# Side products between the score blocks, weighted sums in pairs: reordering one tile of an adaLN attention and expert block

## What is computed

```python
h = _layernorm(x) * (1 + ca) + sa
x = x + ga * _L0_attn_ref(h, Wqkv, bqkv, Wo, bo)          # 16 heads of 8 channels
h = _layernorm(x) * (1 + cb) + sb
x = x + gb * _L0_ffn_ref(h, router_w, expert_weights)     # 8 experts, the best 2 per token

# attention: qkv is reshaped (not transposed) to (B, 16, S, 24)
scores = jnp.einsum('bhsd,bhtd->bhst', q, k) * (1.0 / math.sqrt(hd))
attn = jax.nn.softmax(scores, axis=-1)
vals = jnp.einsum('bhst,bhtd->bhsd', attn, v)
# experts: all eight products are formed, the two best are weighted and summed
out = ((combined + remap_bias) * weights).sum(axis=0)
```

## Time and profile before

| what | value |
|---|---|
| median of 3 runs | 594.01 us (593.64 to 594.24) |
| the profiled execution: its own time | 592.45 us |
| its span, first to last instruction | 590.7 us |
| TensorE busy | 542.7 us, 92% |
| ScalarE busy | 487.3 us, 83% |
| VectorE busy | 341.5 us, 58% |
| GpSimd busy | 219.3 us, 37% |
| mean granted TensorE clock | 0.98 |

### The profile page before, as it was taken

The page is one execution under the profiler, slowest core; times in us unless marked ns, Lnnn a source line. Parts: engine busy times, 40 slices in busy tenths (PEclk is TensorE's granted clock), DMA queues, the critical chain, the costliest instruction groups (busy, mean ns, idle before and its releaser), DMA issues.

```text
span 590.7 us, 14331 instructions
## 1 busy us (share of the span) xinstructions
PE 542.7 (92%) x4046; PEld 202.0 (34%) x4046; DVE 341.5 (58%) x1276; ACT 487.3 (83%) x546; POOL 219.3 (37%) x436
## 2 busy tenths in 40 slices
PE   7499999999999999999999999999999999999944
PEld 5233323333333333333333333333333323333222
DVE  4325566656566666656565656556656666554564
ACT  1389998989888989998989899898989898989700
POOL 1103333333344432343444433333444333433347
PEclk9999999999999999999999999999999999999966
DMA  4383333333233333332233333332333332322000
GB/s 96 96 221 80 80 92 93 84 90 86 70 79 87 85 89 85 90 79 72 72 87 87 85 85 91 83 75 69 85 87 83 85 94 71 85 72 78 22 18 13
DMA packets 85496, 48.43 MB, mean 82 GB/s; under 512 B 61508, under 2 KB 76240, under 8 KB 85456
## 3 DMA queue, kind: packets, MB, share of 16 engines
q1 hardware_dynamic: 84400, 47.43, 31.9%
q10 hardware_dynamic: 1056, 0.46, 0.4%
HBM read 32.91 MB, written 14.94 MB: 81 GB/s over the span
## 4 chain that ended last, share of the span: by engine, by line
PE 59%; ACT 18%; DVE 9%; issue 7%; SPq 2%; POOL 2%; DVEq 2%; DMA 1%; POOLq 0%; ACTq 0%
PE ps_attn L673 20%; ACT probs L522 18%; PE ps_scores L655 16%; PE ps_side L703 9%; PE ps_side L590 4%; DVE sums_inv L980 2%; PE ps_side L597 2%; DVE attn L974 1%; PE ps_side L686 1%; DVE weighted L1060 1%; PE ps_side L584 1%; PE ps_side L682 1%; DVEq L949 1%; PE ps_side L606 1%; PE ps_side L690 1%
## 5 line engine op out<-in xcount | busy, mean ns | idle before, releaser
L522 ACT ACTIVATE probs<-ps_scores 128x1024 f32<-128x1024 f32 x512 | 482.6, 1030 | 68.4 <-PE ps_scores L655 66.2
L673 PE MATMUL ps_attn<-probs,values 128*32 128x512 f32 x2048 | 273.8, 607 | 2.9 <-DVE attn L974 2.9
L655 PE MATMUL ps_scores<-query_stack,key_stack 32*128 32x512 f32 x1024 | 133.5, 500 | 17.7 <-ACT probs L522 4.1
L655 PEld LDWEIGHTS ps_scores<-query_stack,key_stack 32*128 32x128 f32 x1024 | 51.7, 183 | 172.1 <-ACT probs L522 139.8
L411 POOL TENSOR_SCALAR var_eps<-moments 128x1 f32<-128x1 f32 x64 | 12.3, 193 | 247.4 <-DVE moments L991 222.2
L703 PE MATMUL ps_side<-experts_gated,h2T 128*128 (+2 forms) x228 | 75.6, 413 | 0.0
L673 PEld LDWEIGHTS ps_attn<-probs,values 128*32 128x32 f32 x2048 | 40.6, 108 | 67.6 <-issue 57.0
L913 DVE TENSOR_TENSOR qkT<-ps_side,bqk_cols 128x256 f32<-128x256 f32 x32 | 13.6, 425 | 58.8 <-PE ps_side L703 46.5
L1060 DVE TENSOR_TENSOR weighted<-ps_side,coef 128x128 f32<-128x128 f32 (+1 forms) x114 | 46.5, 407 | 1.4 <-PE ps_side L703 1.4
L974 DVE COPY attn<-ps_attn 128x512 f32<-128x512 f32 x32 | 22.1, 691 | 38.3 <-PE ps_attn L673 37.6
L936 DVE TENSOR_REDUCE norm_max<-ps_side 128x1 fp32r<-128x32 f32 x31 | 5.9, 191 | 63.7 <-PE ps_side L703 61.1
(11 more groups left out here) (119 smaller groups left out, 503.0 us busy)
## 6 DMA issues: line engine op xcount, KB each, us to landing
key_stack<-k_scr SPq DMA_DIRECT2D x128, 128.0 KB, 2.7
query_stack<-q_scr SPq DMA_DIRECT2D x124, 64.0 KB, 2.3
q_scr<-qk_parts SPq DMA_DIRECT2D x186, 32.0 KB, 2.0
k_scr<-qk_parts SPq DMA_DIRECT2D x64, 64.0 KB, 1.7
a_scr<-attn SPq DMA_DIRECT2D x128, 18.0 KB
sums<-a_scr SPq DMA_DIRECT2D x32, 64.0 KB, 2.1
attnT<-a_scr SPq DMA_DIRECT2D x32, 64.0 KB, 2.3
out_dram<-out_all SPq DMA_DIRECT2D x32, 64.0 KB, 1.7
```

What stands on the lines that cost most here:

```text
L522: nc.scalar.activation(probs[:, k % RING, g, :], ps_scores[:, slot(parity, k, g), :], ACT.Exp, scale=SCALE)\
L655: mm = nc.tensor.matmul(out_, key_stack[p0:p0 + 32, parity, 2 * k:2 * k + 2, :].rearrange("p j r -> p (j r)"), query_stack[p0:p0 + 32, par ...
L673: mm = nc.tensor.matmul(ps_attn[q:q + 32, :], values[:, parity, g, k, :], probs[:, k % RING, g, h * HALF:(h + 1) * HALF], start=(k == 0), ...
```

## The change

It changes the order in which TensorE goes through a tile, and what depends on that order:

- scores(0) stand alone at the start; then for k = 0, 2, 4, 6: the side group, scores(k+1), both weighted sums k-2 and k-1, and scores(k+2). The side groups thus stand behind the scores of even blocks, and two `weigh` follow each other behind those of odd ones.
- the values of a tile are projected in side1 and no longer in side2 (`a_project_v` with the bank's second quarter), and VectorE reads them there.
- the experts are in four pieces of two.
- on VectorE `c_save` moves from the start of the tile to behind `c_router_top`, and `c_vals` from its end to ahead of the readers of side3.
- on ScalarE the router's exponential comes behind block 0 and no longer behind block 1.

```diff
-    PIECES = ((0, 1), (1, 3), (3, 5), (5, 8))
+    PIECES = ((0, 2), (2, 4), (4, 6), (6, 8))
...
-                    if k == 1 and before >= 3:
+                    if k == 0 and before >= 3:
                         router(plus(act, t, -2))
...
                 if past < 2 <= before:
                     c_transpose(ps, at[-1])
+                if before >= 2 and after >= 1:
+                    a_project_v(at[2], 1 - parity, P)
...
-            def two_blocks(at, parity, before, k0, exact):
-
-                for k in (k0, k0 + 1):
-                    scores(at[0], at[1], parity, k, exact)
-                    if k >= 2:
-                        weigh(at[0], at[1], parity, k - 2)
+            def between_sides(at, parity, before, k, exact):
+
+                scores(at[0], at[1], parity, k, exact)
+                for past_k in (k - 3, k - 2):
+                    if past_k >= 0:
+                        weigh(at[0], at[1], parity, past_k)
                     elif before:
-                        weigh(at[-1], at[0], 1 - parity, KT - 2 + k)
+                        weigh(at[-1], at[0], 1 - parity, KT + past_k)
+                if k + 1 < KT:
+                    scores(at[0], at[1], parity, k + 1, exact)
...
                 with pe.Else():
                     pe.sem_inc(m_scores, M_PE)
-                for k0 in range(0, KT, 2):
-                    with pe.If(flag == 0):
-                        two_blocks(at, parity, before, k0, True)
-                    with pe.Else():
-                        two_blocks(at, parity, before, k0, False)
-                    if k0 == 0:
+                    scores(at[0], at[1], parity, 0, False)
+                for k in range(0, KT, 2):
+                    if k == 0:
                         drained3(at, before, after, 0)
                         side0(ps_side, at, batch, parity, before, after, 0)
...
+                    with pe.If(flag == 0):
+                        between_sides(at, parity, before, k + 1, True)
+                    with pe.Else():
+                        between_sides(at, parity, before, k + 1, False)
...
-                if past < 1 <= before:
+                if after < 0 and past < 1:
                     c_save(t)
...
                 if past < 3 <= before:
                     c_router_top(at[-2])
-
-                written1(at, before, past)
+                if after >= 0 and before:
+                    c_save(t)
+
+                written1(at, before, after, past)
...
                 if after >= 2:
                     a_qk_parts(at[2], at[3])
+                if after >= 0 and before:
+                    c_vals(t)
```

More of the change, by code:

```diff
@@ L591, in a_project_qk, with a_project_v @@
                 mm.then_inc(ev["qk_ps_done"], 1)
-            def a_project_v(u1, ring):
+            def a_project_v(u1, ring, col):
                 for n in range(G):
                     for odd in range(2):
-                        mm = nc.tensor.matmul(ps_side[odd * R:(odd + 1) * R, 2 * P + n * R:2 * P + (n + 1) * R],
+                        mm = nc.tensor.matmul(ps_side[odd * R:(odd + 1) * R, col + n * R:col + (n + 1) * R],
                                               hT[:, ring, n * R:(n + 1) * R], wvT[:, odd].rearrange("p k d -> p (k d)"),
@@ L746, in drained1 @@
                     reached(pe, ev["h2T_done"], at[-1])
+                if before >= 2 and after >= 1:
+                    reached(pe, ev["values_done"], at[2])
                 if past < 4 <= before:
@@ L753, in side2 @@
                     a_project_qk(at[3], parity)
-                if after >= 1:
-                    a_project_v(at[2], 1 - parity)
+                if before < 2:
+                    a_project_v(at[2], 1 - parity, 2 * P)
                 if past < 3 <= before:
@@ L803, in tile @@
                     exact_maxima(t, parity)
+                    scores(at[0], at[1], parity, 0, True)
                 with pe.Else():
                     pe.sem_inc(m_scores, M_PE)
-                for k0 in range(0, KT, 2):
-                    with pe.If(flag == 0):
-                        two_blocks(at, parity, before, k0, True)
-                    with pe.Else():
-                        two_blocks(at, parity, before, k0, False)
-                    if k0 == 0:
+                    scores(at[0], at[1], parity, 0, False)
+                for k in range(0, KT, 2):
+                    if k == 0:
                         drained3(at, before, after, 0)
                         side0(ps_side, at, batch, parity, before, after, 0)
-                    if k0 == 2:
+                    if k == 2:
                         drained0(at, before, after, 0)
@@ L1069, in written0, with written1 @@
                     reached(dve, ev["normT_done"], at[2])
-            def written1(at, before, past):
+            def written1(at, before, after, past):
                 if past < 4 <= before:
                     reached(dve, experts_done[3], at[-3])
+                elif before >= 2 and after >= 1:
+                    reached(dve, ev["v_ps_done"], at[2])
             def written2(at, before, after, past):
@@ L1079, in written2 @@
                     reached(dve, experts_done[0], at[-2])
-                elif after >= 1:
+                elif before < 2:
                     reached(dve, ev["v_ps_done"], at[2])
+                elif after >= 2:
+                    reached(dve, ev["qk_ps_done"], at[3])
             def written3(at, before, after, past):
@@ L1134, in tile @@
                     c_weigh(banks[1], at[-3], parity, 3)
+                if before >= 2 and after >= 1:
+                    a_values(at[2], 1 - parity, P)
                 if past < 3 <= before:
@@ L1142, in tile @@
                     a_qk(at[3])
-                if after >= 1:
-                    a_values(at[2], 1 - parity)
+                if before < 2:
+                    a_values(at[2], 1 - parity, 2 * P)
                 if past < 3 <= before:
```

12 lines of the change are left out of this document (6 added, 6 removed).

## The result

The change makes the kernel faster: 586.23 us (median of 4 runs, 586.05 to 587.36) against 594.12 us (4 runs of before, 593.64 to 596.58) beside it. The ratio is 0.9863, with an interval of 0.9833 to 0.9893. The profiled execution took 587.36 us, the longest of the four, and its span is 585.6 us.

The account below looks back on a forecast made before the run. TensorE and ScalarE hold each other up in turn, so a chain bounds the kernel. Twelve turns at 0.81 (9.7) plus 1.1 for tiles 28 and 29 make 10.8 off 594.01: 583.2 us, range 579 to 588 (0.45).

Parts of the forecast that it names:

- The chain of a pair, 1.62 + 2.29: TensorE and ScalarE: even scores to odd 1.62 unless the side group exceeds 1.19, odd to even 2.29; a pair 3.91.
- the rival of the cheap switch: TensorE: second weigh passes to scores in 0.86, not 1.00, giving 571 us; larger gain, 567 to 579, had chance 0.22.
- The copy: Copy out of `ps_attn` behind VectorE's router chain: weigh(0) at 6.24 (odd) and 7.00 (even), costing 0.28 in odd tiles.
- Head 1 and the register instructions: Even tile's first step: ScalarE's late head 1 makes it 1.84, register instructions behind scores(0) add 0.32, giving 2.16.
- Side1: TensorE's side group with the value projection added and one expert fewer: 1.14 long, hidden under ScalarE's first head.
- What stays hidden: Claimed x1hat ready for side1 (4.8 against 4.88 in even tiles), side2's inputs in time, and `c_vals` waiting up to 1 us.
- Side2: TensorE's side group without the value projection, one expert more: 1.26 long, so its step is 1.69, 0.07 over 1.62.
- The turn: One loop turn of two tiles: odd 15.99 plus even 16.75, 32.74 against 33.55, 0.81 less.
- Tiles 0 to 3, 30 and 31 ... I take nothing there: Tiles outside the loop with smaller side groups: no gain counted, with 1.5 us either way.
- The sum of the transfer's times: SyncE writes `attn` at 7, issues the last read at 10.5, has it at about 13; `c_vals` waits up to 1.
- VectorE idle at `c_vals` for over 2 us with hT late: Sign on VectorE listed as showing the forecast wrong: waiting over 2 us for the values' transfer, delaying hT.
- the small gain: VectorE itself behind, copy up to 0.4 later in the mean, each 0.1 costing 2.8 us: 588 to 593, chance 0.16.

Follow-up runs that it names:

- Number 8: The changed kernel with the copy out of `ps_attn` early, `c_vals` last and side1's value projection ahead of its transpose: 573.53 us, ratio 0.9629; repeated, 574.21 us.
- Number 2: The changed kernel with the copy out of `ps_attn` moved right behind x1hat, ahead of the router's chain on VectorE: 579.63 us, ratio 0.9733.
- number 6: The changed kernel with the copy early and `c_vals` last, all 32 tiles written out instead of the loop: 590.75 us, ratio 0.9922.
- number 9: Number 8 with five register instructions for wait counts moved ahead of scores(0) in the loop's tiles: 571.74 us, ratio 0.9599; repeated, 570.88 us.
- number 1: The changed kernel with `c_vals` back at the end of VectorE's tile, behind side3's readers: 582.41 us, ratio 0.9785.
- number 5: The changed kernel with the copy out of `ps_attn` behind x1hat and `c_vals` at the end of VectorE's tile: 577.86 us, ratio 0.9705.
- number 10: Number 9 with the store of the results issued from GpSimd's queue instead of SyncE's: 570.90 us, ratio 0.9612.

## Why the prediction was right, and where it was not

Predicted was 583.2, measured 586.23. Step by step:

- **The chain of a pair, 1.62 + 2.29: right.** Number 8 has these two steps everywhere in the loop but at the start of an even tile. The second `weigh` takes 1.00 up to the scores and not 0.86, so the rival of the cheap switch falls. By the Trainium skill, page "TensorE: Matmul & The Clock Gate", "Step-by-step: what each phase is for", a drain hides under the next fill, and by the prediction's estimate from it the step over two `weigh` would be 2.15; none in the loop is under 2.28, so at this change of tile shape the measurement decides, and the overlap is not a full one.
- **The copy: its time right, its price too high.** weigh(0) was forecast 6.24 and 7.00 after the tile's start; it came at 6.16 (308.28 to 314.44) and 7.07 (324.11 to 331.18). Number 2 takes the wait away and gains what it cost, 0.10 and 0.34, where 0.28 and 0.50 had been forecast. The rest of the gap was filled by the longer side1 of the next point, so the time of weigh(0) came out right although both terms were off.
- **Head 1 and the register instructions: right.** Forecast 1.84 and 2.16 for the first step, seen 1.83 to 1.85 (tile 28, numbers 6 and 9) and 2.14 to 2.19.
- **Side1: 0.13 too small.** 1.27 and not 1.14: a transpose ahead of the values costs 0.26 and not the 0.13 it took ahead of an expert in the earlier trace rows. In even tiles "What stays hidden" was wrong on `x1hat` too: side1 starts at 5.06 and not 4.88, because `c_x1` comes at 2.40 and not 2.26, and the step is 1.87. Both lie under the wait for the copy and cost the change nothing; they show only once the copy is early. Side2 was 0.08 too large (316.73 to 317.91, 1.18), so step 4 to 5 is 1.62 and not 1.69.
- **The turn: 0.81 less was forecast, 0.97 came.** The odd tile is 15.83 against 15.99, the even one 16.75 as forecast.
- **"What stays hidden": wrong for `c_vals`,** and with it the term "Tiles 0 to 3, 30 and 31 ... I take nothing there". The sum of the transfer's times was right for the loop, where `c_vals` waits 0.64 at 320.65. It was carried over to the tiles around it. From 91 to 103.5 us SyncE issues without a wait and writes `attn` 2.6 after the copy is done, and `attnT` then lands 1.3 later after its issue than in the loop; `c_vals` waits 3.81, and all the readers of side3 with it. To tile 6 this and the smaller groups at the start cost 4.9 where 0.8 was to be gained, 4.2 of it gone in number 1. Tiles 28 to 30 cost 0.8 where 1.1 was to be gained. The prediction had this case among the signs that would make it wrong ("VectorE idle at `c_vals` for over 2 us with hT late"), with its price among those of the small gain, but gave no tile for it. In tiles 1, 2 and 4 and from 28 to 30 `c_vals` waits 2.5 to 5.1.

That 583.2 is only 3.0 us from the result is thus partly luck. The loop gave 1.7 us more than was forecast for its 11 turns from tile 6 on (10.56 against 8.9), and the tiles around it cost 5.5 where 1.9 was to be gained. Between the two profiled executions the gain is 5.1, less than half of the 10.8 in the sum; between the medians it is 7.9. A small slip besides: the list of ranges gives faster 0.83 and slower 0.12, the sentence behind it 0.82 and 0.13.

What stays open: why in each execution other tiles have the late transfer. That SyncE's issues take longer in tiles 2 to 5 (the six of `q_scr` 4.5 us at 90.96, 3.86 in the loop) goes with instructions that run for the first time, as told under number 6; whether fetching them is the cause was not tested.

## What to carry to other kernels

When two engines hold each other up in turn, sum the chain around one round of both, and put optional work where that chain has room: here the same side groups, moved under the first head's exponential, were free up to 1.19 us, and only what goes beyond that was paid. An instruction that waits for a transfer belongs behind everything on its queue that others wait for, even if in the steady state its wait is short: the tiles at the start and the end have other slack. It is no cure, since side0 needs its result anyway (late first steps in numbers 5, 6 and 9). And a sequencer's register instructions count when they stand behind a matmul that the next step follows at once; computed ahead of that matmul they cost a fifth.

## What the runs showed of the hardware

- **A wait can be paid twice.** In tile 5 of the change TensorE waited 2.04, its granted clock then fell to 0.58 of full, and the step behind took 3.23 instead of 2.29. In tile 31 of number 9 (its second run) it waited 1.45, the clock was 0.50 from 522 to 525 us, and the step behind took 3.97, two `weigh` in it 3.60 instead of 1.92. But in tile 29 of the change it waited 1.48, the clock stayed at 1.00, and the step behind was 2.29. And in tile 30 of number 5 two idle stretches of 0.48 and 0.36, 1.0 us apart, were followed by a clock of 0.50 (513 to 516 us) and a step of 3.87. So a wait can cost nothing more, or 0.9 to 1.7 us on top; what decides between them no run here tells. The waits of up to 0.6 at the copy never showed it: from 128 to 487 us the mean clock is 1.00.
- **The order of shapes in a group has a price.** One 128x128 transpose takes 0.13 to 0.16 ahead of an expert's matmuls and 0.26 ahead of the 64-column value projection.
- **Issuing transfers can be the bound.** SyncE's round of 23 issues, 0.3 to 0.6 us each, takes about 15.4 us in the loop (15.78 a tile in number 9, of which it waits 0.4 for `qk_parts`), with the transfers themselves at a third of the engines' time. Of the 15.4 it spends 1.1 waiting for the write of `attn` to land.
- **An issue can take longer the first time its instructions run.** In the second and later turns of the loop none of the change's 308 issues that write `q_scr` or read keys and queries took more than 0.62 us; elsewhere some took up to 1.69, and up to 2.24 in number 6, where the tiles are written out.
- **Landing.** From issue to landing `attnT` took 2.2 us in the median, the store of the results 1.6 when issued by SyncE and 2.0 when issued by GpSimd (number 10). The Trainium skill, page "DMA: Bandwidth & Descriptors", "Anatomy of one DMA — SWDGE (gpsimd) path", gives some 2.0 us as the fixed cost of a transfer that GpSimd issues, and number 10's trace agrees with it.
